# Where in a step TensorE sums the gathered table rows: at the step's end, or between its exponents and its dense product

## The reference

```
q = (x @ Wq).reshape(b, n, HEADS, DIM) * DIM ** (-0.5)
kv_scores, indices = _pk(x, Wq_pk, pk_keys)      # 16 best of 64 x 64 keys per head, softmax of their scores
ind = indices + offsets
k = einsum('bnhk,bnhkd->bnhd', kv_scores, keys_table[ind])
v = einsum('bnhk,bnhkd->bnhd', kv_scores, values_table[ind])
sim = einsum('bihd,bjhd->bhij', q, k)            # causal, softmax
out = einsum('bhij,bjhd->bhid', attn, v) ... @ Wo
```

## Time and profile before

| what | us |
|---|---|
| median of 3 runs (lowest, highest) | 7210.47 (7197.34, 7213.68) |
| the profiled execution, its own time | 7216.25 |
| its span in the trace | 7214.4 |
| mean granted TensorE clock over the span, share of full | 0.765 |
| the attention's steady part, by the trace | 1313 to 7150 |

### The profile page before, as it was taken

The page is one execution under the profiler, slowest core; times in us unless marked ns, Lnnn a source line. Parts: engine busy times, 40 slices in busy tenths (PEclk is TensorE's granted clock), DMA queues, the critical chain, the costliest instruction groups (busy, mean ns, idle before and its releaser), DMA issues.

```text
span 7214.4 us, 93389 instructions
## 1 busy us (share of the span) xinstructions
PE 5504.2 (76%) x24068; PEld 3410.1 (47%) x24068; DVE 4381.4 (61%) x16725; ACT 2250.2 (31%) x5719; POOL 3144.6 (44%) x3416
## 2 busy tenths in 40 slices
PE   4566671578887878787878788888788888888879
PEld 2344430345554545454545455454455555554546
DVE  6666656665666666666665656575757575756522
ACT  2333330223332323232323333333333233333323
POOL 0011103455555455555454545454555555555541
PEclk7555565778787878887878787888888878788877
DMA  1000001122122222221222122212122212221210
GB/s 32 0 0 0 0 12 51 46 56 59 55 62 57 60 57 62 57 61 52 61 56 61 55 59 57 61 56 63 54 61 56 61 53 61 57 60 54 59 56 23
DMA packets 157848, 353.82 MB, mean 49 GB/s; under 512 B 71716, under 2 KB 75812, under 8 KB 156968
## 3 DMA queue, kind: packets, MB, share of 16 engines
q0 software_dynamic: 96912, 200.25, 10.5%
q1 hardware_dynamic: 60440, 147.74, 6.7%
HBM read 345.04 MB, written 4.61 MB: 48 GB/s over the span
## 4 chain that ended last, share of the span: by engine, by line
PE 34%; another core or an unknown queue 19%; DVE 15%; issue 12%; ACT 4%; DVEq 0%; DMA 0%; ACTq 0%; POOLq 0%
PE ps L945 34%; DVE topi L1340 2%; DVE w L1526 2%; DVE top L1334 2%; ACT ex L1203 1%; DVE sc L1346 1%; DVE idxf L1502 1%; DVE hot L1493 1%; DVE hot L1498 1%; DVE left L1304 1%; DVE eq L1471 1%; DVE cs L1346 1%; DVE wmat L1518 1%; DVE eq L1463 0%
## 5 line engine op out<-in xcount | busy, mean ns | idle before, releaser
L937 POOL DMA_INDIRECT rows<-table_dram,idxT x3024 | 3060.5, 1012 | 2923.8 <-PE ps L945 1660.5
L1526 DVE SCALAR_TENSOR_TENSOR w<-ps,ex 128x750 f32<-128x750 f32 x1024 | 958.8, 936 | 1950.1 <-remote 912.7
L945 PE MATMUL ps<-w,dtab 128*128 128x375 f32 x4096 | 1837.6, 580 | 5.5 <-issue 5.4
L945 PEld LDWEIGHTS ps<-w,dtab 128*128 128x128 f32 x4096 | 920.0, 232 | 486.0 <-issue 259.7
L1203 ACT ACTIVATE ex<-ps 128x750 f32<-128x750 f32 x1024 | 818.5, 799 | 716.6 <-PE ps L945 386.7
L945 PE MATMUL ps<-rank_dense,half 128*128 128x375 bf16 x1920 | 539.8, 368 | 493.6 <-DVE w L1526 346.0
L945 PEld LDWEIGHTS ps<-wmat,rows 128*128 128x128 f32 x6048 | 786.5, 207 | 138.9 <-issue 87.3
L945 PE MATMUL ps<-wmat,rows 128*128 128x8 f32 x6048 | 790.7, 265 | 57.8 <-issue 41.5
L945 PE MATMUL ps<-parts,half 128*128 128x375 bf16 x2048 | 611.7, 374 | 261.0 <-ACT ex L1203 169.7
L945 PEld LDWEIGHTS ps<-rank_dense,half 128*128 128x128 bf16 x1920 | 186.2, 109 | 1010.4 <-DVE w L1526 518.7
L1217 ACT COPY kvg<-ps 128x28 f32<-128x28 f32 x432 | 80.0, 185 | 1378.3 <-remote 823.6
(11 more groups left out here) (206 smaller groups left out, 7015.4 us busy)
## 6 DMA issues: line engine op xcount, KB each, us to landing
dtab<-dense_dram SPq DMA_DIRECT2D x256, 512.0 KB
rows<-table_dram,idxT POOLq DMA_INDIRECT x3024
xin<-x_dram SPq DMA_DIRECT2D x16, 187.5 KB
half<-halves_dram POOLq DMA_DIRECT2D x1, 1828.0 KB, 13.0
rows_in<-hh SPq DMA_DIRECT2D x16, 93.8 KB, 2.2
rows_in<-uu SPq DMA_DIRECT2D x16, 93.8 KB, 2.2
u_front<-rows_in SPq DMA_DIRECT2D x16, 93.8 KB
h_now<-rows_in SPq DMA_DIRECT2D x16, 93.8 KB
```

Source lines behind the costliest of these rows:

```text
L937: nc.gpsimd.indirect_dma_start(out=rows[:, t, :], out_offset=None, in_=table[:, :], in_offset=bass.IndirectOffsetOnAxis(ap=idxT[:, c, t:t ...
L945: return nc.tensor.matmul(out_, lhsT, rhs, start=start, stop=stop, skip_group_check=open_bank)
L1526: nc.vector.scalar_tensor_tensor(w[:, p % 2, :, :], ps[:, 2:4, 0:T], float(K), ex[:, p % 2, :, :], ALU.is_gt, ALU.mult).then_inc(s_w, 1)
```

## The change

In step p of PE, the meals are taken out of the loop over the small units and put between `exponent(p+1)` and `product(p-1)`. All other units stay where they are. No instruction is added or taken away, and the code of the other engines is the same, so ACT still copies a meal in its next step and POOL still issues the same DMAs in the same order.

```
                     exponent(*following)
+                for name, i in here(0, p, kind) + here(1, p, kind):
+                    if name == "eat":
+                        gathered(i, kind, n)
                 if p >= 1 and kind != "epilogue":
                     product(n, p - 1)
...
                     if name == "part" and i >= 2:
                         part(i, kind, n)
-                    if name == "eat":
-                        gathered(i, kind, n)
```

## The result

The changed kernel takes 7524.8 us (median of 4 runs, 7466.76 to 7527.74), the kernel before 7203.91 us beside it (4 runs, 7184.83 to 7213.68). The ratio is 1.042, with a 95% interval of 1.038 to 1.046: 4.2% slower. The profiled execution took 7526.39 us, with a span of 7524.6 us.

A forecast was written before the change was run, and what follows sets the result against it. PE was taken to bound the kernel. Bank waits +69, freed slots and copies -30, DVE 0 made +39 us against the profiled 7216.25; on the median 7210.47, 7249 us, 0.5% slower; 8-in-10 range 7080 to 7385.

The forecast's parts named there:

- What bounds the kernel: Attention: PE, busy 81%, sets the pace where it runs without a gap; its gaps cost twice, since its clock falls behind them.
- 138 us in all, ... I take half: All meals' bank waits, 8.6 us a batch; half reaches the end, 69 us, the rest caught up in PE's idle time.
- The bank, meals behind a `sim`: Six meals a batch wait for DVE's mask without product and ranks as cover: 0.9 us each, 5.4 us a batch.
- The middle of three cases: Loss per meal behind a `sim`: 0, 0.9 (meal 18) or 1.6 us (meal 11); 0.9 taken for each of six.
- The bank, meals behind ACT's copies: Thirteen meals a batch behind `turn_probs` or `score` wait 0.25 us each for ACT's copy: 3.2 us a batch.
- Meals behind another meal: Six meals a batch follow in their bank a meal that has moved as much: they cost nothing.
- The freed slots: Meals signal 1.6 us earlier to ACT's copy and POOL's next group: -30 us, ends 0 and -198 us.
- What DVE sees: Ranks come 1.6 us later at a step with a meal, earlier at the next: 0, within 40 us either way.
- the product without cover: Clearly slower: product runs behind the mask instead of while PE waits for `w`; +206 us, 7416 us, chance 0.12.
- A meal escapes a late signal: Faster: meal 15 signals before the late signals begin, PE's 7.12 us wait goes; 7050 to 7150 us, chance 0.38.
- The long stalls changed places: Sign named beforehand: if stalls of more than 5 us change places, the prediction is wrong in kind.
- The clock: Sign: granted clock in the attention stays at 0.80 to 0.81; 0.83 or more would speak for a faster kernel.

The follow-up runs named there:

- meal behind the ranks: Against the kernel before, each meal goes right behind the ranks of its step, ahead of the other small units; ratio 1.002.
- wide meals: Kernel before's order, each meal's seven matmuls of 8 columns replaced by two of 504, sums of gathered rows left out; 0.991 of the kernel before.
- split meal: Against the kernel before, matmuls 1 to 3 of a meal go between the product's two matmuls, 4 to 7 behind the ranks; ratio 1.043.
- mixed orders: Kernel before with seven or ten chosen meals moved between product and ranks or behind the next step's exponents; 1.006 and 1.017 beside 7222 us.
- meal in the next step: Against the kernel before, each meal goes behind the exponents of the next step, ahead of its product; 1.014, and 1.008 when repeated.
- wide kernel with six meals moved: Against the kernel before, meals 0, 1, 19, 21, 25, 26 ahead of the product, all meals two matmuls of 504 columns; 0.988, and 1.018 beside 7222 us.

## Why the prediction was wrong

The sign was right, and for the reason given, the meals' waits for their bank; the time, 7249 us, and the range, up to 7385, were not. Step by step:

- *What bounds the kernel.* PE paces it and its gaps cost twice, said the text, and then the sum counted each gap once. This is the step that failed: "138 us in all, ... I take half". The waits themselves were more than twice as long, 304 us of new idle time ahead of meals, and not half of it was absorbed but nearly all, by other stalls that shrank: PE's idle time grew by 19 us. What the sum put at nothing is the clock. Behind these gaps meal, product and ranks run at the lower clock: of the 292 us that the table's stretch grew by, 259 are the clock's, and nine tenths of those follow such gaps.
- *The bank, meals behind a `sim`.* Sized at 6 x 16 x 0.9 = 86 us (its own figures for meal 18, 2277.2 against 2276.22, give 0.98). Measured, from the timeline, 135 us of idle time with late signals and 147 without. The middle of three cases was taken, and the wait was bounded by the product and ranks that had covered it. But the wait lasts until DVE has done its slices, whatever was moved: 1.8 to 3.6 us at meals 11 and 18 in the rows above.
- *The bank, meals behind ACT's copies.* Sized at 13 x 16 x 0.25 = 52 us, and 24 measured without late signals, so a copy that is on time was not priced too low. With late signals it was 195 us, 136 of them at meal 7. The prediction had this very copy in view and put it into the upper end only. Meals behind another meal, taken as free, had 31 us, all at meal 26.
- *The freed slots.* -30 us. PE's wait for `kvg` fell from 81.7 to 32.5 us, and the rhythm of the copies at meals 1 to 4 stayed, 10.8, 11.5 and 10.2 us apart in the third batch. This part was right.
- *What DVE sees.* Taken as 0 within 40 us. PE's wait for `w` grew by 49 us. The other direction was not counted: the ranks, queued behind a waiting meal, are what DVE's `w` stands for (4.62 us at meal 11). Without late signals `w` waits 1212 us for PE, against 571 with the meal behind the ranks.
- *The rivals.* The clearly slower one, "the product without cover", was the mechanism, at a chance of 0.12 and 7416 us. Its price was short in the clock's term: 31 us for one product in four, where 259 were measured. The clock falls for the meal too, and for the ranks. "A meal escapes a late signal" did not come about. (Its own terms give 7035 to 7115, a little under the 7050 to 7150 that it states.) The long stalls changed places, which the text had named as a sign of being wrong. Stalls over 5 us between two products were 40 before (428 us), mostly at steps 24, 35 and 58, and are 43 after (390 us), mostly at steps 16, 35 and 60.
- *The clock* was said to stay at 0.80 to 0.81, and is 0.79. The mean looks almost right because it mixes two things that moved against each other: PE's busy time at the lower clock grew from 1536 to 2054 us, and its idle time there fell from 505 to 319.
- *Luck.* That the measured time is not further off is owed to the late signals: in the comparison without them the same change costs twice the share.

The Trainium skill, "TensorE: Matmul & The Clock Gate", "Part 1: The HAM clock gate", says that the clock is set "based on how busy the PE has been recently". For gaps the rows agree, as at meal 18. But the clock also fell where PE had no gap: in the kernel with the meal behind the ranks, 70 of 111 falls in the table's stretch came with a meal just run and no gap of half a microsecond (93 if one looks back less far), and the wide meals took the falls to 26.

What stays open: why the signals of PE are late in some comparisons and not in others; why the clock stays down longer with the split meal; and the mixed orders without late signals, and the meal in the next step with them.

## What to carry to other kernels

A wait that is moved to the front of a queue can cost more than its own length: what is queued behind it runs late and, on TensorE, slower, and the engine that it waits for may next wait for it. Without late signals 172 us of idle time ahead of meals went with 484 us more. Ask of a moved matmul what now lies ahead of it and behind it: a covered wait was worth some 7% here, and wide work instead of two narrow pieces side by side 3 to 5%. When idle time hardly grows while the time does, compare the busy time of the same instructions. And take the granted clock over busy time alone, since the mean over a stretch mixes idle time into it.

## What the runs showed of the hardware

- TensorE's clock falls without a gap. Behind 8-column meals and other small matmuls, with the exponents alone between two meals, it went to the lower of its two levels while PE was busy all the time: meal 1.72 us, next meal 2.99, product 2.85 instead of 1.43. With two matmuls of 504 columns instead of seven of 8, the clock's loss in the same order fell from 393 to 34 us.
- The same program took 5690 or 7220 us, 27% apart, with all runs of one comparison alike, and on one chip both. In the slower case ACT, DVE and POOL wait for PE with nothing in the profile that holds them (the longest such wait is 23.6 us, for DVE's `w`, in the wide kernel with six meals moved). Where POOL was issuing a group of indirect DMAs, ACT's copy of a meal came 1.6 to 2.3 us after the group's last one (third batch of the changed kernel, meals 1 to 4). In the other case POOL issues as many and no wait lacks a name. What sets it was not found.
